# Two down products of a gated MLP, moved one pass later in three of sixteen passes

## The chip, the cores and the metric

One Trainium2 chip, one of its cores. TensorE (PE, its weight loads PEld), VectorE (DVE), ScalarE (ACT), GpSimd (POOL) and SyncE (SP) each run their own list of instructions in order and wait for each other through semaphores. The metric is the device time of one execution, in microseconds (us).

## The reference

`x` and `ctx` are (16, 256, 512): 16 batches of 256 tokens, width 512.

```python
x = x + tanh(g_xattn) * mlstm(layernorm(x), ctx, ctx, ...)   # 8 heads, decay matrix per head
h = layernorm(x)
scores = softmax(h @ router_w.T); top 2 of 16 experts
y = sum over the two experts of gate * ((silu(h @ Wg[e]) * (h @ Wu[e])) @ Wd[e])
s = (silu(h @ shared_gate) * (h @ shared_up)) @ shared_down  # 512 -> 512 -> 512, all tokens
x = x + tanh(g_ffn) * (y + s)
```

The change concerns `s`, the shared expert, and in it the last product, by `shared_down`.

## The kernel before

The kernel has three phases. In the first (to about 600 us) the 16 batches go through a software pipeline of passes; in the second (to about 1027 us) 79 tiles of 128 routed rows go through the experts; in the third the expert results are gathered and added, and the shared expert of the "late" batches is computed.

Pass `t` of the first phase works on four batches at once: F = t+1 (turn the context and x, gate rows), A = t (the attention of its 8 heads: `spread`, `scores_pair`, `pv`), G = t-1 (second layer norm, `turn`, router) and H = t-2 (ranks and slots of the routing, and the shared expert). The order is written out by hand in a function `step` for each engine, so every engine's instruction list is fixed. On PE a pass begins with `scores_pair(A, 0)` and has the sixteen gate products (`gates_pe`, L1030) about in its middle; I call what lies ahead of them the first half of the pass and what lies behind them the second half, and count times from them.

The shared expert of one batch is four `shared(b, m)` (24 matmuls of 128x256 each, L1125; they need DVE and ACT behind them for silu) and two `shared_down(b, j)` (12 matmuls of 128x512 each, L1136, one for each 128 tokens; DVE adds the result to `base_out`, L1618). Each product has three terms, since the operands are split in a high and a low part. `shared(b, 0)` and `(b, 1)` stand at the end of pass b+1, `(b, 2)` and `(b, 3)` in the first half of pass b+2, and both `shared_down` in the second half of pass b+2.

Batches 9, 11, 13 and 15 are `LATE`: their shared expert is left for the third phase. So passes 11, 13, 15 have no `shared(H, 2)`, `shared(H, 3)` and no `shared_down`, and passes 10, 12, 14 have no `shared(G, 0)`, `shared(G, 1)`. `EARLY` is all other batches, `LAST` = 14, `SH` numbers the early ones. Behind pass 15 stands a `drain`.

All products of the shared expert but `shared(b, 1)` and one of batch 14 use PSUM bank 7 (`FF`); `shared_down(b, 1)` waits until DVE has read `shared_down(b, 0)` out of it, and `shared(next, 0)` until DVE has read both. `spread(A, h)` waits until ACT has made the decay of head h-2, `pv(A, h)` until DVE has multiplied scores and decay (L1455), `columns` (L1042) until DVE has copied the logits. DVE's list has, in the first half of a pass: `h_stats(G)`, heads 0 and 1, `keep(H, 1)`, `norm_front(F, 0)`, `shared(H, 2)`, `center(G)`, heads 2 and 3, `x2_add`, `out_pair(A, 0)`, `norm_front(F, 1)`, `shared(H, 3)`, `x2_stats(G)`, top, heads 4 and 5, and `post_norm(G)` (L1525, for which PE's `turn(G, 0)` waits).

Of the kernel before, what the change touches and what calls it, by code (L numbers as in the profile page):

```python
# [44 lines left out]
LATE = (9, 11, 13, 15)  # L45
EARLY = tuple(b for b in range(B) if b not in LATE)
SH = {b: n for n, b in enumerate(EARLY)}
LAST = EARLY[-1]
LATE_TILES = len(LATE) * ST
YRING = 4  # L50
LATE_LOADS = [9, 16]
# [33 lines left out]
def flamingo_kernel(nc, x, ctx_in, g_xattn, g_ffn, igate_w, igate_b, fgate_w, fgate_b, ln_scale,  # L85
# [10 lines left out]
    with ExitStack() as stack:  # L96
# [163 lines left out]
        def gu_bank(b, m):  # L260
            return MB[0] if b == LAST and m == SC - 1 else GU[m]

# [714 lines left out]
        def _(pe):  # L977
# [135 lines left out]
            def shared(b, m):  # L1113
                pe.wait_ge(shared_in.sem, shared_in.upto(SHARED_PIECES - 1))
                pe.wait_ge(x2lo_made.sem, x2lo_made.upto(b.n))
                if m == 0:
                    pe.wait_ge(base_made.sem, base_made.upto(SH[b.n] - 1))
                elif b.n == LAST and m == SC - 1:
                    pe.wait_ge(decay_made.sem, decay_made.upto(B - 1))
                elif m > 1:  # L1120
                    pe.wait_ge(sh_act_made.sem, sh_act_made.upto(SH[b.n], 1 if m == 2 else 3))
                for at, w in ((0, sh_gate), (S, sh_up)):
                    for c in range(DC):
                        for p, (w_part, x_part) in enumerate(PARTS):
                            last = mm(gu_bank(b.n, m)[:, at:at + S], w[:, w_part, c, m * P:(m + 1) * P], x2nT[:, x_part, c, :],  # L1125
                                      start=(c + p == 0), stop=(c == DC - 1 and p == 2))
                last.then_inc(sh_made.sem, 1)
# [17 lines left out]
            def step(t, front=True, attend=True, route=True, rest=True):  # L1145
                F, A, G, H = t + 1, t, t + -1, t + -2
                inner, rest = rest, rest and H.n in SH
                mix = route and G.n in SH
                if attend:
                    scores_pair(A, 0)  # L1150
                    spread(A, 0)
                    spread(A, 1)
                if rest:
                    shared(H, 2)
                if front:
                    turn_ctx(F, 0)
                if attend:
                    spread(A, 2)
                    spread(A, 3)
                    pv(A, 0)  # L1160
                    pv(A, 1)
                    scores_pair(A, 1)
                if front:
                    turn_ctx(F, 1)
                if rest:
                    shared(H, 3)
                if front:
                    turn_x(F, 0)
                if attend:
                    spread(A, 4)  # L1170
                    spread(A, 5)
                    scores_pair(A, 2)
                if front:
                    turn_x(F, 1)
                if attend:
                    pv(A, 2)
                    pv(A, 3)
                if front:
                    gates_pe(F)
                if attend:  # L1180
                    spread(A, 6)
                    spread(A, 7)
                if route:
                    turn(G, 0, front)
                if rest:
                    shared_down(H, 0)
                if inner and route:
                    rank(H, front, attend)
                if attend:
                    pv(A, 4)  # L1190
                    pv(A, 5)
                if route:
                    turn(G, 1, front)
                if rest:
                    shared_down(H, 1)
                if attend:
                    scores_pair(A, 3)
                if route:
                    router(G, front)
                if mix:  # L1200
                    shared(G, 0)
                if attend:
                    pv(A, 6)
                    pv(A, 7)
                if route:
                    logits_pe(G)
                if mix:
                    shared(G, 1)
                if front:
                    columns(F, route)  # L1210
# [146 lines left out]
        def _(dve):  # L1357
# [237 lines left out]
            def shared(b, m):  # L1595
                dve.wait_ge(sh_tanh_made.sem, sh_tanh_made.upto(SH[b.n], m + 1))
                dve.wait_ge(sh_lo_made.sem, sh_lo_made.upto(SH[b.n], m - 1))
                v.scalar_tensor_tensor(sh_act[:, m % 2, :], silu_t[:, :], 1.0, gu_bank(b.n, m)[:, 0:S], ALU.add, ALU.mult
                                       ).then_inc(sh_silu_made.sem, 1)
                dve.wait_ge(sh_silu_made.sem, sh_silu_made.upto(SH[b.n], m + 1))  # L1600
                v.scalar_tensor_tensor(sh_act[:, m % 2, :], sh_act[:, m % 2, :], 0.5, gu_bank(b.n, m)[:, S:2 * S],
                                       ALU.mult, ALU.mult).then_inc(sh_act_made.sem, 1)
# [39 lines left out]
            def step(t, ahead=True, front=True, attend=True, route=True, rest=True, split=False):  # L1642
                N, F, A, G, H = t + 2, t + 1, t, t + -1, t + -2
                inner, rest = rest, rest and H.n in SH
                mix = route and G.n in SH
                if route:
                    h_stats(G)
                if attend:
                    head(A, 0)
                    head(A, 1)  # L1650
                if rest:
                    keep(H, 1)
                if split:
                    piece(0)
                if front:
                    norm_front(F, 0)
                if rest:
                    shared(H, 2)
                if route:
                    center(G)  # L1660
                if attend:
                    head(A, 2)
                    head(A, 3)
                if split:
                    piece(1)
                if route:
                    x2_add(G)
                if attend:
                    floor(A)
                    out_pair(A, 0)  # L1670
                if split:
                    piece(2)
                if front:
                    norm_front(F, 1)
                if split:
                    piece(3)
                if rest:
                    shared(H, 3)
                if route:
                    x2_stats(G)  # L1680
                if rest:
                    keep(H, 2)
                if inner and route:
                    top(H)
                if attend:
                    head(A, 4)
                    head(A, 5)
                if split:
                    piece(4)
                if route:  # L1690
                    post_norm(G)
                if attend:
                    out_pair(A, 1)
                if rest:
                    keep(H, 3)
                if split:
                    piece(5)
                if front:
                    read_gates(F)
                if inner and route:  # L1700
                    choose(H)
                if route:
                    turn(G, 0)
                if ahead:
                    stats(N)
                if rest:
                    shared_down(H, 0)
                if inner and route:
                    rank(H)
                if attend:  # L1710
                    out_pair(A, 2)
                if route:
                    turn(G, 1)
                if front:
                    rows(F)
                if rest:
                    shared_down(H, 1)
                if inner and route:
                    slots(H)
                if attend:  # L1720
                    head(A, 6)
                    head(A, 7)
                if front:
                    rows_end(F)
                if mix:
                    shared(G, 0)
                if route:
                    keep_logits(G)
                if attend:
                    out_pair(A, 3)  # L1730
                if mix:
                    keep(G, 0)
                    shared(G, 1)
                if front:
                    columns(F)
                if inner and route:
                    weigh(H)
# [215 lines left out]
```

## Time and profile before

| | us |
|---|---|
| median of 3 runs (lowest, highest) | 1143.31 (1141.41, 1145.24) |
| profiled execution, device time | 1135.05 |
| its span | 1133.2 |
| PE busy | 1025.1 (90%) |
| DVE busy | 761.3 (67%) |
| ACT busy | 386.4 (34%) |
| POOL busy | 419.3 (37%) |
| mean granted clock of PE | 0.949 |

The share of PE in the chain that ended last is 80%. Shares over the whole span say little of three passes of 34 us each; what counts is what the engines wait for in passes 10 to 15, at 402.9 to about 583 us. The granted clock of PE has two levels, 1.00 (2.4 GHz) and 0.50 (1.2 GHz); a stretch in which it changes shows a value between them.

### The profile page before, as it was taken

The page shows a single profiled execution, that of the slowest core. Times are in us where ns is not written, and L with a number is a line of the kernel's source. Part 1 is how long each engine was busy: PE and PEld are TensorE (multiplying, and loading weights), DVE is VectorE, ACT ScalarE, POOL GpSimd, SP SyncE. Part 2 cuts the span into 40 slices and gives each one's busy share as a digit, 9 for nine tenths or more (in the row PEclk, how much of TensorE's full clock was granted, in tenths as well). Part 3 has the DMA queues.
Part 4 walks back from the last instruction along what each step waited for, and adds up shares of the span by engine and source line. Part 5 has one row for each costly group of instructions (what it writes and reads, how often), then busy time and mean ns, then how long its engine had stood idle before and what let it go on. Part 6 is the DMA issues. An engine that isn't in the chain of part 4 may idle for free.

```text
span 1133.2 us, 20738 instructions
## 1 busy us (share of the span) xinstructions
PE 1025.1 (90%) x6395; PEld 859.9 (76%) x6395; DVE 761.3 (67%) x1983; ACT 386.4 (34%) x854; POOL 419.3 (37%) x309
## 2 busy tenths in 40 slices
PE   4689999999999988989895599999999999999882
PEld 2578988898889877868684478888888888887661
DVE  2888889888888887878766544444444444444766
ACT  2644444444443444435421123233323333231010
POOL 4010221222112221222215536558656676204675
PEclk9889999999999998989976899999999999999986
DMA  7340210222012202120107744564555554836888
GB/s 259 149 164 1 76 71 9 82 75 76 20 56 76 75 38 80 52 94 38 75 38 260 265 135 167 176 207 158 170 195 193 168 176 149 325 112 186 285 288 272
DMA packets 60036, 155.60 MB, mean 137 GB/s; under 512 B 7296, under 2 KB 7296, under 8 KB 58016
## 3 DMA queue, kind: packets, MB, share of 16 engines
q0 software_dynamic: 18448, 69.22, 17.6%
q1 hardware_dynamic: 29008, 62.93, 16.1%
q10 hardware_dynamic: 12480, 22.16, 5.5%
q8 instruction: 59, 0.97, 0.4%
q14 instruction: 41, 0.34, 0.1%
HBM read 93.46 MB, written 60.82 MB: 136 GB/s over the span
## 4 chain that ended last, share of the span: by engine, by line
PE 80%; DVE 5%; issue 4%; DMA 4%; POOL 3%; ACT 2%; SPq 1%; ACTq 0%; POOLq 0%; DVEq 0%; another core or an unknown queue 0%
PE bank L1260 19%; PE bank L1125 12%; PE bank L1278 10%; PE bank L1030 5%; PE bank L1136 5%; PE bank L1053 4%; PE bank L993 4%; PE bank L1248 3%; POOL w_ring L694 3%; PE bank L1074 3%; PE bank L1077 3%; PE bank L1075 3%; PE bank L1322 2%; PE bank L1062 2%; PE bank L1269 2%
## 5 line engine op out<-in xcount | busy, mean ns | idle before, releaser
L1260 PE MATMUL bank<-w_ring,x2nT 128*128 x948 | 241.8, 404 | 1.7 <-DVE x2nT L1829 1.7
L1260 PEld LDWEIGHTS bank<-w_ring,x2nT 128*128 128x128 f32 x948 | 174.3, 191 | 37.7 <-issue 2.4
L1125 PE MATMUL bank<-x2nT,w_ring 128*128 128x256 f32 x1152 | 148.5, 285 | 0.0
L563 POOL DMA_INDIRECT routed_x<-x2n,slot_u x64 | 65.8, 1029 | 222.8 <-DVE slot_u L1593 207.0
L1125 PEld LDWEIGHTS bank<-x2nT,w_ring 128*128 128x128 f32 x1152 | 141.0, 191 | 0.3
L1811 DVE SCALAR_TENSOR_TENSOR ctxT<-ctxT,bank 128x256 f32<-128x256 f32 x79 | 33.3, 421 | 138.7 <-ACT ctxT L921 138.7
L1278 PE MATMUL bank<-w_ring,sh_actT 128*128 x474 | 123.7, 396 | 1.1 <-DVE sh_actT L1824 1.1
L648 POOL TENSOR_TENSOR w_ring<-area,one 128x3072 fp32r<-128x3072 f32 x14 | 74.2, 5303 | 115.5 <-PE bank L1278 115.5
L1278 PEld LDWEIGHTS bank<-w_ring,sh_actT 128*128 128x128 f32 x474 | 88.9, 188 | 22.5 <-issue 1.4
L651 POOL TENSOR_TENSOR w_ring<-area,w_ring 128x3072 fp32r<-128x3072 f32 x14 | 95.6, 6832 | 2.5 <-POOL w_ring L648 2.5
L921 ACT ACTIVATE ctxT<-bank 128x256 f32<-128x256 f32 x79 | 30.3, 384 | 189.9 <-PE bank L1260 189.9
L694 POOL DMA_INDIRECT w_ring<-routed_y,y_slot x64 | 66.5, 1039 | 34.9 <-issue 19.6
L1136 PE MATMUL bank<-w_ring,sh_actT 128*128 128x512 f32 x288 | 75.2, 411 | 1.3 <-issue 1.3
L1455 DVE SCALAR_TENSOR_TENSOR area<-bank,area 128x384 f32<-128x384 f32 x128 | 66.0, 551 | 14.5 <-PE bank L1053 7.8
L927 ACT COPY cs_in<-bank 128x512 f32<-128x512 f32 x79 | 46.3, 586 | 84.7 <-PE bank L1278 79.1
L1822 DVE CAST sh_actT<-bank 128x256 fp32r<-128x256 f32 x79 | 33.5, 424 | 60.9 <-PE bank L1269 60.9
L570 POOL TENSOR_TENSOR x_rstd<-x_var,minus_half 128x2 f32<-128x2 f32 x16 | 12.8, 797 | 152.4 <-DVE x_var L1518 152.4
L1053 PE MATMUL bank<-area,ctxT 64*128 64x256 f32 (+1 forms) x512 | 67.1, 379 | 0.0
L778 ACT ACTIVATE area<-bank,key_log 128x256 f32<-128x256 f32 x128 | 61.1, 478 | 10.8 <-PE bank L1064 10.2
L1136 PEld LDWEIGHTS bank<-w_ring,sh_actT 128*128 128x128 f32 x288 | 53.8, 194 | 13.0 <-issue 1.5
L1248 PE MATMUL bank<-ident,x2n 128*128 128x128 f32 x316 | 48.4, 277 | 12.5 <-issue 7.0
L1053 PEld LDWEIGHTS bank<-area,ctxT 64*128 64x128 f32 x512 | 51.0, 206 | 11.3 <-issue 5.5
(224 smaller groups left out, 2052.8 us busy)
## 6 DMA issues: line engine op xcount, KB each, us to landing
routed_y<-cs_in ACTq DMA_DIRECT2D x79, 256.0 KB, 2.3
x2n<-routed_x SPq DMA_DIRECT2D x75, 256.0 KB, 2.9
base_out<-in_x_dram SPq DMA_DIRECT2D x16, 512.0 KB, 5.0
cs_in<-in_ctx_dram SPq DMA_DIRECT2D x16, 512.0 KB, 4.0
area<-n_L_ffn_expert_gate_dram POOLq DMA_DIRECT2D x16, 512.0 KB, 4.7
area<-in_L_ffn_expert_up_dram POOLq DMA_DIRECT2D x16, 512.0 KB, 6.3
area<-n_L_ffn_expert_down_dram POOLq DMA_DIRECT2D x16, 512.0 KB, 7.7
out_dram<-base_out SPq DMA_DIRECT2D x32, 256.0 KB
```

The source lines that it names most:

```text
L563: pool.indirect_dma_start(out=routed_x, in_=x2n[:, b.par, j, :], in_offset=None, out_offset=bass.IndirectOffsetOnAxis(ap=slot_u[:, b.par, ...
L648: g.tensor_tensor(w_ring[:, k, 0, :], stage[k], one[:, :].to_broadcast([P, EW]), ALU.mult).then_inc(expert_hi_in.sem, 1)
L651: g.tensor_tensor(w_ring[:, k, 1, :], stage[k], w_ring[:, k, 0, :], ALU.subtract).then_inc(expert_in.sem, 1)
L694: pool.indirect_dma_start(out=y_in[k][:, c, :], in_=routed_y, out_offset=None, in_offset=bass.IndirectOffsetOnAxis(ap=y_slot[:, at:at + 1] ...
L778: s.activation(decay[:, k, 0:S], MB[k][:, 0:S], ACT.Exp, bias=key_log[:, b.par, 0, h:h + 1], scale=-1.0)
L1053: last = mm(QK[k][:, at:at + n], ctxT[half, b.par, q, frm:frm + P], xnT[half, b.par, q, S - n:S], start=True, stop=True)
L1125: last = mm(gu_bank(b.n, m)[:, at:at + S], w[:, w_part, c, m * P:(m + 1) * P], x2nT[:, x_part, c, :], start=(c + p == 0), stop=(c == DC - ...
L1136: last = mm(FF[:, :], sh_actT[:, x_part, m, j * P:(j + 1) * P], sh_down[:, w_part, m, :], start=(m + p == 0), stop=(m == SC - 1 and p == 2))
L1248: last = tr(bank[t.par][:, c * P:(c + 1) * P], xt[:, k, c * P:(c + 1) * P], ident[:, :])
L1260: last = mm(bank[2 + t.par][:, :], xtT[:, x_part, t.par, c * P:(c + 1) * P], w_gu[:, bass.ds(slot, 1), w_part, c, :].rearrange("p a i -> p ...
L1278: last = mm(bank[5 + t.par][:, :], act_aT[:, x_part, t.par, c * P:(c + 1) * P], w_dn[:, bass.ds(slot, 1), w_part, c, :].rearrange("p a i - ...
L1455: v.scalar_tensor_tensor(cmat[:, k, :], QK[k][:, 0:TRI], QK_SCALE, decay[:, k, :], ALU.mult, ALU.mult).then_inc(c_made.sem, 1)
```

## The change

`CARRY` are the early batches whose successor is late, without the last: 8, 10 and 12. Their two `shared_down` leave the second half of pass b+2 (10, 12, 14) and stand in the first half of pass b+3 (11, 13, 15), in the places where `shared(H, 2)` and `shared(H, 3)` stand in a pass whose H is early. PE's list and DVE's list are changed in the same way; ACT, POOL and SP are not.

```diff
+CARRY = tuple(b for b in EARLY if b + 1 in LATE and b != LAST)
 # PE, step
                 if rest:
                     shared(H, 2)
+                if t.n - 3 in CARRY:
+                    shared_down(H + -1, 0)
                 if front:
                     turn_ctx(F, 0)
...
                 if rest:
                     shared(H, 3)
+                if t.n - 3 in CARRY:
+                    shared_down(H + -1, 1)
                 if front:
                     turn_x(F, 0)
...
-                if rest:
+                if rest and H.n not in CARRY:
                     shared_down(H, 0)
...
-                if rest:
+                if rest and H.n not in CARRY:
                     shared_down(H, 1)
 # DVE, step
                 if rest:
                     shared(H, 2)
+                if t.n - 3 in CARRY:
+                    shared_down(H + -1, 0)
                 if route:
                     center(G)
...
                 if rest:
                     shared(H, 3)
+                if t.n - 3 in CARRY:
+                    shared_down(H + -1, 1)
                 if route:
                     x2_stats(G)
...
-                if rest:
+                if rest and H.n not in CARRY:
                     shared_down(H, 0)
...
-                if rest:
+                if rest and H.n not in CARRY:
                     shared_down(H, 1)
```

## Rows read from the trace of the kernel before

**Rows 1.** Engines by stretch: us, busy (instructions) per engine, PEclk, DMA share, GB/s.
```profile
365.94:402.91 36.97, 36.97 (x292) 32.41 (x292) 32.43 (x95) 16.41 (x39) 7.63 (x9) 1.00 0.16 58
402.91:437.17 34.26, 30.46 (x196) 24.30 (x196) 28.80 (x92) 13.98 (x32) 8.21 (x9) 0.85 0.26 93
437.17:471.38 34.21, 31.59 (x267) 28.12 (x268) 27.67 (x83) 16.11 (x38) 6.58 (x7) 1.00 0.14 48
```
**Rows 2.** Chain that ended last: start us, us, engine, tile, line.
```profile
392.51 0.44 PE bank L993 x4
...
402.91 3.58 PE bank L1030 x16
...
407.61 2.81 PE bank L1136 x12
...
437.17 3.58 PE bank L1030 x16
...
539.89 3.58 PE bank L1030 x16
```
**Rows 3.** Timeline, pass 10 behind its gate products: start us, us, instruction, idle before.
```profile
413.72 0.42 DVE L1417 SCALAR_TENSOR_TENSOR f_row<-gates,f_row 8x256 f32<-8x256 f32 x1
...
415.94 0.71 DVE L1618 SCALAR_TENSOR_TENSOR base_out<-bank,tanh_g,base_out 128x512 f32<-128x512 f32 x1
...
418.07 0.44 PE L1074 MATMUL bank<-area 128*128 128x65 f32 x2 [0.92 <-DVE area L1455]
...
420.65 0.28 PE L1042 MATMUL bank<-ident,key_max 40*128 40x40 f32 x2 [0.48 <-DVE logits L1530]
...
422.24 0.61 PE L993 MATMUL bank<-ident,cs_in 128*128 128x128 f32 x4
```
**Rows 4.** Timeline, pass 11 behind its gate products.
```profile
446.06 0.58 ACT L728 CAST x2nT<-bank 128x512 fp32r<-128x512 f32 x1
...
447.40 0.41 DVE L1417 SCALAR_TENSOR_TENSOR f_row<-gates,f_row 8x256 f32<-8x256 f32 x1
447.42 1.20 PE L1100 MATMUL bank<-x2nT,router_wT 128*128 128x256 f32 x8 [2.12 <-DVE x2nT L1613]
```
**Rows 5.** Engines by stretch, columns as in Rows 1: where PEclk falls, holds and returns.
```profile
422.00:426.00 4.00, 2.32 (x25) 1.93 (x23) 3.87 (x11) 2.64 (x8) 3.65 (x5) 1.00 0.51 152
442.00:446.00 4.00, 2.94 (x28) 2.54 (x28) 3.67 (x14) 3.92 (x8) 0.00 (x0) 1.00 0.00 0
426.00:436.00 10.00, 9.28 (x48) 7.59 (x48) 7.38 (x24) 3.77 (x10) 0.69 (x1) 0.51 0.54 207
...
562.00:566.00 4.00, 4.00 (x24) 3.48 (x23) 1.76 (x3) 1.35 (x4) 0.27 (x1) 0.59 0.00 0
582.00:586.00 4.00, 4.00 (x31) 4.00 (x30) 0.74 (x2) 0.36 (x1) 2.82 (x3) 0.85 0.32 129
```
**Rows 6.** Chain that ended last, single products at either clock.
```profile
400.19 0.85 PE bank L1053 x8
...
427.14 1.58 PE bank L1053 x8
...
609.98 1.02 PE bank L1109 x4
...
1087.65 4.94 PE bank L1322 x12
```
**Rows 7.** Timeline, pass 15.
```profile
566.13 1.02 DVE L1455 SCALAR_TENSOR_TENSOR area<-bank,area 128x384 f32<-128x384 f32 x2 [2.37 <-PE bank L1053]
...
573.85 1.12 PE L993 MATMUL bank<-ident,x2n 128*128 128x128 f32 x4
...
575.91 0.67 PE L1074 MATMUL bank<-area 128*128 128x65 f32 x2
...
578.50 1.06 PE L993 MATMUL bank<-ident,x2n 128*128 128x128 f32 x4
...
581.08 2.07 PE L1100 MATMUL bank<-x2nT,router_wT 128*128 128x256 f32 x8
```

## The prediction

> **What bounds the kernel now.** I read the page first: PE is busy for 90% of the span and has 80% of the chain. That holds for the passes with all products: pass 9 to 10 (from one block of gate products to the next) takes 36.97 us with PE busy in all of it at clock 1.00 [rows 1]. Then I cut the span at the gate products, which the chain shows once in each pass [rows 2]. From pass 10 to 11 it takes 34.26 us, PE is busy for 30.46 of them, and the mean clock is only 0.85; from 11 to 12 it takes 34.21 us at clock 1.00 [rows 1]. (12 to 13 and 13 to 14 repeat these two to 0.1 us.) Nearly 12 us of PE work are absent in the first of them (four `shared`), and the time is shorter by only 2.7 us. So in the stretch that the change touches PE alone is not the bound: it waits for ACT and DVE in the second half of pass 10, and in the first half of pass 11 it runs 10 us at 1.2 GHz.
>
> All times below are counted from the gate products of pass 10 (402.91), 11 (437.17) and 14 (539.89), each called g.
>
> **Second half of passes 10, 12, 14: the products leave.** Two `shared_down`, 2.81 us each [rows 2], and two additions of DVE, about 0.7 us each [rows 3], go. What is late next is already in the trace: the second half of pass 11 has no down products. There the second turn of x2n waits for ACT (its cast begins at g+8.89), the router for DVE after 2.12 us of idleness, and DVE begins `rows` at 447.40, g+10.23 [rows 4]; in pass 10 it is 413.72, g+10.81 [rows 3]. So of 5.62 us of PE work taken away, 0.58 us come out. Behind that DVE has the scans, the second addition of the down product, slots and heads 6, 7; without the addition (0.65 us of it beyond the scan that it overlaps) `pv(6)` starts at 15.16 - 0.58 - 0.65 = g+13.93 instead of g+15.16 (418.07) [rows 3]. That is 1.23 us, and all that this half can give. PE idles for the rest: 2.1 us ahead of the router, as in rows 4, and then from the router's end (g+11.45) to g+13.93, another 2.5 us.
>
> At clock 1.00 `pv(6)` to `columns` is 420.65 - 418.07 = 2.58, and `columns` to the end of `spread(1)` 422.24 - 420.65 = 1.59 [rows 3], so `shared_down(8, 0)` would begin at g+18.1.
>
> **The clock.** It fell at about 426.2 in the kernel before. What PE did ahead of it: from 422 to 426 it was busy for 2.32 us of 4.00. From 442 to 446 it was busy for 2.94 of 4.00, and the clock held [rows 5]. In the changed pass 10 the stretch g+8 to g+14 has only the router in it, 1.2 us of some 5.9: much sparser than the one behind which the clock fell, and it comes 10 us earlier, in the second half where products were taken away. I therefore expect the fall at g+10 to g+13, and the return in the solid work of scores, spreads and the down product; it was back 10 us after the fall last time, and after 20 us in pass 15 (562 to 583) [rows 5].
>
> What stands ahead of the down product then runs at 1.2 GHz. A pair of `pv` takes 578.50 - 575.91 = 2.59 us, the logits 1.02, with 0.46 from them to `columns` 4.07 in all instead of 2.58. `scores_pair` takes 1.58 instead of 0.85, two spreads about 1.1 (twice the 0.5 left of the 1.59, an estimate), `columns` 0.3: 3.0 instead of 1.59 [rows 3, 6, 7]. So the first down product begins at 13.93 + 4.07 + 3.0 = g+21.0. It takes 2.81 us at 2.4 GHz; at 1.2 GHz the nearest row, 12 products of 128x512 that ran mostly at 0.50, has 4.94 [rows 2, 6]. Its end E is between g+23.8 and g+25.9; I take the middle between a return at its start and one at its end, a little to the early side since scores and spreads ahead of it are solid too: E = g+24.7.
>
> **First half of passes 11 and 13: the products arrive.** In pass 9, from the end of `shared(H, 2)` (392.51) to the gate products (402.91) it takes 10.40 us, bound by PE all the way, with `shared(H, 3)` in the place that the second down product now takes, of the same length [rows 2]. DVE's additions (0.7 us each) replace two silu steps and a `keep` of 0.4 each there, so DVE stays behind PE as in pass 9. The next gate products begin at 24.7 + 10.4 = g+35.1, against g+34.26: **+0.8 us**, bounds -0.1 (E = 23.8) and +2.0 (E = 25.9). Twice, for batches 8 and 10: +1.6.
>
> **Pass 15.** No F there, so it is not bound by PE work but by DVE and by PE at half clock. Now DVE's heads 2 and 3 begin at 566.13, g+26.24. Afterwards: E = 24.7, two spreads 0.6, a pair of `pv` 1.33, `scores_pair(1)` 0.85 and 0.2 to DVE give g+27.7, 1.46 later. From there DVE's list to `post_norm` (573.85 for PE's turn, 7.72 later) gets one addition more, 0.71: turn(G, 0) at g+36.1 instead of 33.96, +2.2. Behind it PE went at 1.2 GHz to the router at 581.08 [rows 7], and since PE again waits for DVE between g+33.4 and g+36.1 I keep that. So **+2.2 us**, bounds +1.3 and +3.4, and if these last 9.3 us ran at full clock 2.6 less (half of pv, turn, scores and router), so -1.3. The drain hangs on it one for one.
>
> **Hidden or free.** Nothing waits for `base_out` of 8, 10, 12 before `shared(next, 0)`, which comes 11 us behind the gate products of pass 11. ACT's `keep(10, 0)` waits for both downs of batch 8 and stands behind them too. No DMA is added or moved: context and x for two passes on are released by turns in the first half as in pass 9, and no instruction of POOL or SP is passed. If that cover were gone, the cost would be the whole of a load, 4 to 5 us; pass 9 has the same order and no such wait.
>
> **Sum.** 0.8 + 0.8 + 2.2 = +3.8 us on the profiled 1135.05, 1138.9. The profiled execution is 8.26 us under the median of the runs; the difference is carried over: 1143.31 + 3.8 = **1147.1**. With all bounds of these terms: -0.1 - 0.1 - 1.3 = -1.5 to 2.0 + 2.0 + 3.4 = +7.4, so 1141.8 to 1150.7.
>
> **Rivals.**
> *The clock holds (faster).* Then the first down begins at g+18.1, E = 20.9, the next gate products at g+31.3: -2.95 us, twice. In pass 15 heads 2 and 3 begin at g+23.9, 2.3 earlier, minus the addition 0.7: -1.6. Together -7.5, **1135.8**. For it speaks that the clock held over 2.12 us of idleness in pass 11 [rows 4]; against it that the dense `shared(G, 0)` followed there at once, while here 2.5 us more of idleness follow. It decides at the fall: it must not come before the first down.
> By the Trainium skill (TensorE: Matmul & The Clock Gate, "Part 1: The HAM clock gate") the array is throttled behind a stretch of idleness and released by sustained activity. Taken at its word, gaps that always have a router or a pair of `pv` between them would not throttle it, and this rival's 1135.8 would be the time; the trace disagrees, since the clock fell with PE busy for 2.32 of 4.00 us.
>
> *The fall comes, but the clock is back before the down product (same).* E = 23.8, each of the two passes -0.1, pass 15 +1.3: **1144.4**. Scores and spreads (2.7 us at half clock) would have to be enough to bring it back; in rows 5 PE was busy for 9.28 of 10 us before it came back, which speaks against it, but it comes back somewhere in such work.
>
> *The clock stays down past the first down (slower still).* Then turn, spreads, pv, scores and turn behind it take 3.5 us more, half of the second down 1 us: E = 25.9 and 4.5 on it, +6.5 for each of two passes, and pass 15 +3.4 + 2.5: +19, **1162**. Against it: five us without a gap.
>
> **How the numbers follow.** The forecast has 0.62, the clock back early 0.18, the clock holding 0.14, the long stay 0.06. A measurement of this kernel can tell about 0.3%, 3.4 us, from no change. The forecast lies just above that bound: of its 0.62 I put 0.35 above and 0.27 within. Slower 0.35 + 0.06 = 0.41; same 0.27 + 0.17 = 0.44; faster 0.14 + 0.01 = 0.15. Where the clock falls hangs on how gaps happen to lie in an execution, so the case before may itself move by a us or two; the range takes in the rival that is faster, nearly, and the upper bound with 1 us more: 1137 to 1152.
>
> **What would show it.** Right: in the changed kernel `pv(6)` of pass 10 at g+13.9; a clock of 0.50 from about g+10..13 to about g+23; the first L1136 of pass 11 at g+21 and over 3 us long; gate products of pass 11 at g+35.1; heads 2, 3 of pass 15 at g+27.7. Wrong: PEclk 1.00 between g+8 and g+18 (the first rival), or the gate products of pass 11 under g+33.

## The result, and the profile after

The changed kernel takes 1146.72 us in the median of 20 runs (1143.19 to 1154.82), the kernel before in the same series 1143.41 (1138.49 to 1151.49). The ratio is 1.0041, 95% interval [1.0021, 1.0061]: +4.7 us, between +2.4 and +7.0 (the two medians are 3.3 us apart). The forecast was 1147.1, +3.8 us. The profiled execution of the changed kernel took 1151.72 us, its span is 1149.9 us. It is 16.7 us over the profiled execution of before, and most of that is not the change: its gate products of pass 10, up to which nothing is changed, come 4.6 us later already, and 7 us come behind the router of pass 15. So here too the stretches between gate products are compared, not the spans. Line numbers are a little higher in the changed kernel: its L1032, L1102 and L1138 are L1030, L1100 and L1136 of before, and DVE's are six higher.

Engines by stretch, after, columns as in [rows 1]: gate products of pass 10 to those of 11, then 11 to 12, 12 to 13, 13 to 14.

```profile
407.46:442.98 35.52, 30.83 (x196) 25.34 (x196) 28.45 (x86) 13.68 (x31) 7.57 (x9) 0.81 0.25 89
442.98:477.19 34.21, 31.59 (x267) 28.12 (x268) 28.48 (x88) 16.32 (x39) 7.09 (x8) 1.00 0.14 48
477.19:512.04 34.85, 29.30 (x195) 24.05 (x196) 28.36 (x87) 13.68 (x31) 7.44 (x9) 0.85 0.21 76
512.04:547.74 35.70, 33.09 (x268) 29.61 (x268) 30.39 (x91) 16.31 (x39) 7.50 (x9) 0.95 0.08 31
```

The first stretch was 34.26 us in [rows 1]. It has the same 196 matmuls and now takes 35.52; the clock's mean went from 0.85 to 0.81. The second is unchanged. The fourth is 1.5 us longer than its like in the kernel before, by a short fall of the clock. Such a fall also comes in an execution of the kernel before (below), so this trace alone can't put it down to the change.

Timeline of pass 10 behind its gate products (g = 407.46), after; the answer to [rows 3, 4].

```profile
417.69 0.41 DVE L1423 SCALAR_TENSOR_TENSOR f_row<-gates,f_row 8x256 f32<-8x256 f32 x1
...
417.71 2.08 PE L1102 MATMUL bank<-x2nT,router_wT 128*128 128x256 f32 x8 [2.12 <-DVE x2nT L1619]
...
421.38 0.69 PE L1076 MATMUL bank<-area 128*128 128x65 f32 x2 [1.60 <-DVE area L1461]
...
425.65 0.41 PE L1044 MATMUL bank<-ident,key_max 40*128 40x40 f32 x2 [0.48 <-DVE logits L1536]
...
428.42 2.06 PE L1138 MATMUL bank<-w_ring,sh_actT 128*128 128x512 f32 x4
```

Read it against the forecast: `rows` begin at g+10.23 (forecast g+10.23), `pv(6)` at g+13.92 (13.93), the first down product at g+20.96 (21.0). PE sits idle ahead of the router for 2.12 us and ahead of `pv(6)` for 1.60 (forecast 2.5 at full clock). The router takes 2.08 us instead of 1.20 [rows 4], so the clock was already down.

Engines in 415.46 to 421.46, g+8 to g+14, after.

```profile
415.46:421.46 6.00, 2.29 (x13) 1.86 (x9) 4.77 (x13) 2.87 (x6) 0.00 (x0) 0.66 0.00 0
```

PE was busy for 2.29 of 6.00 us, much of that only because the router ran at half clock. The clock fell at g+9.9 and came back at g+23.6, inside the first down product. In passes 12 and 14 it fell at g+11.9 and g+13.0.

Chain that ended last, after.

```profile
407.46 3.58 PE bank L1032 x16
...
428.67 3.99 PE bank L1138 x12
...
436.44 2.79 PE bank L1138 x12
```

The chain counts a product from the end of the one before it, so the first carried product begins 0.25 us later here (g+21.2) than in the timeline. It takes 3.99 us, the second 2.79. The first ends at 432.66, E = g+25.2 (forecast 24.7), and the gate products of pass 11 follow 10.3 us later (forecast 10.4).

Timeline of pass 15 (g = 547.74), after; the answer to [rows 7].

```profile
575.61 1.02 DVE L1461 SCALAR_TENSOR_TENSOR area<-bank,area 128x384 f32<-128x384 f32 x2 [0.72 <-PE bank L1055]
...
579.10 0.74 DVE L1624 SCALAR_TENSOR_TENSOR base_out<-bank,tanh_g,base_out 128x512 f32<-128x512 f32 x1
...
583.77 0.66 PE L995 MATMUL bank<-ident,x2n 128*128 128x128 f32 x4 [1.71 <-DVE x2n L1531]
...
585.70 0.20 PE L1089 MATMUL bank<-chosen,before_b 128*128 128x16 bf16 x1 [1.28 <-DVE taken_mid L1564]
...
588.43 1.06 PE L995 MATMUL bank<-ident,x2n 128*128 128x128 f32 x4
...
591.00 1.41 PE L1102 MATMUL bank<-x2nT,router_wT 128*128 128x256 f32 x8
```

Heads 2 and 3 begin at g+27.87 (forecast 27.7; before 26.24), `turn(G, 0)` at g+36.03 (forecast 36.1; before 33.96) and waits 1.71 us for DVE. The router begins at g+43.3 instead of g+41.2: +2.1, forecast +2.2. The clock was not down all through this stretch, as it was in the kernel before: it came back at g+23.2 and fell again at g+36.9, behind `turn(G, 0)`, which takes 0.66 us instead of 1.12. The time from `turn(G, 0)` to the router is 7.2 us in both kernels, since PE then waits 1.28 us for DVE.

### The profile page after: what moved, and what is told of

Read it like the earlier page. It is cut to its first block, busy times and chain, and to the rows that moved or that the text cites. A ratio compares the mean times of both kernels' runs of the same rounds, so it can differ in the third digit from the quotient of the medians.

```text
span 1149.9 us, 20738 instructions
## 1 busy us (share of the span) xinstructions
PE 1032.3 (90%) x6395; PEld 865.9 (75%) x6395; DVE 763.5 (66%) x1983; ACT 386.0 (34%) x854; POOL 419.7 (36%) x309
## 4 chain that ended last, share of the span: by engine, by line
PE 79%; issue 6%; DVE 4%; DMA 4%; POOL 3%; ACT 2%; SPq 1%; another core or an unknown queue 0%; ACTq 0%; POOLq 0%; DVEq 0%
PE bank L1266 19%; PE bank L1127 12%; PE bank L1284 9%; PE bank L1138 5%; PE bank L1032 5%; PE bank L1055 4%; PE bank L995 4%; PE bank L1254 3%; POOL w_ring L696 3%; PE bank L1076 2%; PE bank L1077 2%; PE bank L1079 2%; PE bank L1064 2%; DMA routed_x<-xn 2%; PE bank L1328 2%
## 5 line engine op out<-in xcount | busy, mean ns | idle before, releaser
L1266 PEld LDWEIGHTS bank<-w_ring,x2nT 128*128 128x128 f32 x948 | 174.9, 191 | 38.0 <-issue 2.4
L1138 PE MATMUL bank<-w_ring,sh_actT 128*128 128x512 f32 x288 | 77.4, 420 | 1.3 <-issue 1.3
L1138 PEld LDWEIGHTS bank<-w_ring,sh_actT 128*128 128x128 f32 x288 | 55.7, 201 | 13.6 <-issue 1.5
L1076 PE MATMUL bank<-area 128*128 128x65 f32 x256 | 52.0, 287 | 10.9 <-DVE area L1461 10.9
L1254 PE MATMUL bank<-ident,x2n 128*128 128x128 f32 x316 | 48.9, 278 | 13.7 <-issue 7.3
```

The source lines that it names most:

```text
L1076: mm(HO[:, r:r + VW], cmat[:, k, 0:P], v_aug[:, b.par, 0, h, :], start=True, stop=True)
L1138: last = mm(FF[:, :], sh_actT[:, x_part, m, j * P:(j + 1) * P], sh_down[:, w_part, m, :], start=(m + p == 0), stop=(m == SC - 1 and p == 2))
L1254: last = tr(bank[t.par][:, c * P:(c + 1) * P], xt[:, k, c * P:(c + 1) * P], ident[:, :])
L1266: last = mm(bank[2 + t.par][:, :], xtT[:, x_part, t.par, c * P:(c + 1) * P], w_gu[:, bass.ds(slot, 1), w_part, c, :].rearrange("p a i -> p ...
```

## Experiments

Each run's ratio is to the kernel before in runs of the same series, and the microseconds behind it are that ratio worked out on 1143. g is always the block of gate products that opens a stretch.

**Fill the emptied places** (fill_gaps). A helper `fill(n)` issues n matmuls of 128x512 into bank 7, read by nobody.

```diff
+                if rest and H.n in CARRY:
+                    fill(8, acts=H)
                 if route:
                     router(G, front)
+                if rest and H.n in CARRY:
+                    fill(9)
```

> The changed kernel, and in the second half of passes 10, 12, 14 PE gets idle work in the two places where it waits: 8 products of 128x512 ahead of the router and 9 behind it, into bank 7, whose content nobody reads. The output is the same. Theory A (the clock): the change is slow because the emptied second half lets the clock fall at g+10; filled, the clock holds, pv(6) still starts at about g+13.9 to g+14.3, the first down product at about g+18.4 instead of g+21.0, and gate products of pass 11 at g+31.3 to g+32 instead of g+35.5. Pass 15's router ends about 3 us earlier than in the changed kernel. Together 7 to 11 us under the changed kernel, 3 to 7 us under the kernel before. Rival B (the place: DVE's additions and bank 7 delay heads 2 and 3 whatever the clock does): the fillers only add work, the gate products of pass 11 stay at g+35 or later, time as the changed kernel or slower.

Measured: 1141.49 us, ratio to before 0.9963 [0.9933, 0.9994], so -4.2 us, and 8.9 under the changed kernel's ratio. Engines by stretch: 10 to 11, 11 to 12, and g+13.9 to g+21.9.

```profile
411.15:442.57 31.42, 30.02 (x212) 24.05 (x213) 27.80 (x86) 13.80 (x31) 7.81 (x9) 1.00 0.28 102
442.57:478.30 35.73, 33.12 (x268) 29.64 (x268) 30.18 (x89) 16.31 (x39) 7.31 (x8) 0.95 0.12 45
425.00:433.00 8.00, 7.44 (x57) 6.53 (x58) 7.22 (x25) 2.62 (x7) 6.76 (x7) 1.00 0.35 135
```

With 17 more matmuls issued the first stretch takes 31.42 instead of 35.52 us, at clock 1.00 (PE busy for 7.44 of the 8 us behind `pv(6)`), and the first down product begins at g+18.1, where the forecast put it for a clock that holds; that rival had 31.3. Order, places and DVE's work are those of the changed kernel. 12 to 13 takes 31.59 us. So the whole loss in these two stretches, and the gain that was within reach, hang on the clock: shown, and rival B falls. The fillers did not hold the clock everywhere. It fell for 3.4 us at g+10.4 in pass 11 and at g+11.4 in pass 13 (where no fillers stand), and at g+16.7 in pass 14; the router of pass 15 begins at g+40.9, 2.4 us earlier than in the changed kernel, and ends 1.7 us earlier and not the 3 expected.

**The same work in the kernel before** (before_fill). Behind `spread(A, 1)` of passes 11, 13, 15: `fill(12)`.

```diff
                 if rest:
                     shared(H, 2)
+                if t.n - 3 in (8, 10, 12):
+                    fill(12, bases=H + -1)
                 if front:
                     turn_ctx(F, 0)
```

> The kernel before, and in the first half of passes 11, 13, 15, behind spread(1), PE gets 12 products of 128x512 that nobody reads, 2.8 us of work where a down product stands in the changed kernel. Output the same. Theory A: the sparse stretch at g+19 to g+23 is filled and the clock, which fell there at g+23.3, holds; the 10 us at 1.2 GHz become 5 us of work and the rest is bound by DVE; gate products of pass 11 at g+31 to g+32.5 instead of g+34.3, 2 us in each of two passes and 2 to 4 in pass 15: 5 to 8 us under the kernel before, although 8.4 us of work are added. Rival B (the work in the first half is what costs): PE work is added on the path, gate products of pass 11 at g+36 to g+37, 5 to 8 us over the kernel before.

Measured: 1137.50 us, 0.9951 [0.9917, 0.9984], -5.6 us.

```profile
410.74:443.93 33.19, 30.30 (x208) 24.39 (x208) 27.80 (x86) 13.89 (x31) 7.83 (x9) 0.95 0.27 96
478.13:509.76 31.63, 28.73 (x208) 23.19 (x208) 27.82 (x87) 13.89 (x31) 7.71 (x9) 1.00 0.24 84
```

Useless work makes the kernel before faster. Where the clock held throughout, 12 to 13 takes 31.63 us; in 10 to 11 it fell at g+18.1 for 3.4 us and the stretch takes 33.19, over the 32.5 expected. The fall came ahead of the fillers' place, so they could not prevent it.

**One product stays, one goes** (one_late).

```diff
                 if t.n - 3 in CARRY:
-                    shared_down(H + -1, 0)
+                    shared_down(H + -1, 1)
...
                 if mix:
                     shared(G, 0)
+                if rest and H.n in CARRY:
+                    shared_down(H, 0)
                 if attend:
                     pv(A, 6)
```

(the same is done in DVE's list, and the other carried call goes)

> Of the two down products of 8, 10, 12 the first stays in its own pass, but stands behind the router, where shared(G, 0) stands in passes with an early G; only the second goes one pass later, to the place of shared(H, 2). Theory A: the product behind the router fills 2.5 us of idleness, the clock holds or falls at g+10 to g+12 and is back by g+14 since dense work follows (as in the second half of pass 11); pv(6) at about g+14.4; the carried product at g+18.5 to g+19; then 7.6 us of PE work or about 9 of DVE's: gate products of pass 11 at g+30 to g+32.5. 6 to 12 us under the changed kernel, 2 to 7 under the kernel before. Rival B (every carried product costs by its place): half of the loss stays, about 2 us over the kernel before.

Measured: 1135.34 us, 0.9927 [0.9890, 0.9963], -8.4 us. Stretches 10 to 11, 11 to 12 and 13 to 14:

```profile
403.55:435.53 31.98, 27.17 (x196) 22.29 (x196) 28.62 (x86) 13.71 (x31) 7.60 (x9) 0.95 0.29 99
435.53:469.74 34.21, 31.59 (x268) 28.11 (x268) 28.39 (x88) 16.35 (x39) 7.10 (x8) 1.00 0.13 48
502.19:537.84 35.65, 33.03 (x268) 29.56 (x268) 30.37 (x91) 16.34 (x39) 7.50 (x9) 0.95 0.08 31
```

The same 196 matmuls take 31.98 us, with a fall of 3.4 us only (g+9.8 to g+13.2): the clock was back 0.9 us into the product behind the router, where the changed kernel has no product and stayed down to g+23.6. In passes 12 and 14 the clock held there and fell at g+18.7 and g+18.9, again for 3.4 us; 12 to 13 takes 32.45 us. It beats both kernels, by more than expected (2 to 7 us under before, 6 to 12 under the changed one): it is 13.0 us under the changed kernel's ratio.

**Batch 12 alone** (only12). `CARRY = (12,)`.

> CARRY is (12,) alone: passes 10 to 13 are as before, passes 14 and 15 as in the change. By the forecast's terms pass 15 alone costs +2.2 us and each of the other two +0.8; then this kernel is +1 to +2.5 us over the kernel before, the router of pass 15 ends at g+44.5 to g+45.5 (counted from the gate products of pass 14), against g+43.3 in the kernel before, and gate products of pass 11 are at about g+34.3. If pass 15 costs nothing, the router ends at g+43 to g+43.5.

Measured: 1144.54 us, 1.0003 [0.9972, 1.0034], which tells nothing of 2 us. Its stretches do: 10 to 11, and gate products of pass 14 to 43.5 us behind them.

```profile
403.53:435.50 31.97, 27.73 (x196) 21.98 (x196) 27.80 (x86) 13.78 (x31) 7.84 (x9) 0.95 0.27 99
539.80:583.28 43.48, 35.81 (x219) 28.91 (x218) 32.15 (x104) 14.16 (x34) 7.43 (x8) 0.77 0.12 49
```

The router of pass 15 starts at the end of the second stretch, g+43.5, as in the changed kernel, and ends at g+45.0, within the 44.5 to 45.5 expected: the loss of pass 15 comes without the other two. The first stretch was not expected: passes 10 and 11 are those of the kernel before, and take 31.97 us and not 34.26. The clock fell at g+23.5, where it fell at g+23.3 in the first trace of before, but for 3.4 us instead of 10.2.

**Carried products of one matmul** (thin_down). Inside the loop over m of PE's `shared_down`:

```diff
+                    if b.n in CARRY:
+                        if m == SC - 1:
+                            last = mm(FF[:, :], sh_actT[:, 0, m, j * P:(j + 1) * P], sh_down[:, 0, m, :],
+                                      start=True, stop=True)
+                        continue
```

> The changed kernel, but each of the six carried down products does one of its 12 matmuls; the other 11 (with the values that they would add for batches 8, 10, 12) are left out. 2.6 us of PE work less in each place, 15.5 us in all; waits and DVE's additions stay. Theory A (the clock): the product itself was the solid work that brought the clock back; without it the clock, fallen at g+10 to g+13, stays at 0.50 through most of the first half of passes 11 and 13: the product's place is reached at g+21 as before, and the gate products of pass 11 come at g+33.5 to g+36, as late as with the whole products (35.5), if not later. Time within 5 us of the changed kernel. Rival B (what costs is PE work in the first half): gate products of pass 11 at 35.5 - 5.2 = g+30.3, 5 us less in each of three passes, 15 us under the changed kernel, 1131 to 1134.

Measured: 1140.27 us, 0.9983 [0.9951, 1.0015]. Stretch 10 to 11, and g+9.6 to g+23.6 of it:

```profile
407.43:439.38 31.95, 25.99 (x173) 21.25 (x174) 27.61 (x82) 13.80 (x31) 7.40 (x8) 0.79 0.26 99
417.00:431.00 14.00, 11.24 (x56) 9.91 (x57) 11.17 (x32) 4.43 (x10) 6.60 (x7) 0.51 0.31 114
```

And one wait of PE behind the place of the second product:

```profile
437.45 0.66 PE L995 MATMUL bank<-ident,xn 128*128 128x128 f32 x4 [0.77 <-DVE xn L1416]
```

A miss for both. The place is reached at g+21.0 again, with the clock down since g+9.9; but the clock comes back at g+23.6 without the product, as it did with it, so I was wrong that the product is needed for that: what PE did there was turn, spreads and `pv`. The stretch is 3.6 us shorter than with whole products, near the 3.99 us of the first. Nothing comes out for the second: from the end of the first carried product to the gate products it takes 10.2 us, and 10.3 with whole products, since turn and spreads run at half clock up to g+23.6 and PE then waits, here 0.77 us for DVE. The time is 6.6 us under the changed kernel's ratio, more than theory A's 5 and far less than rival B's 15. Of 15.5 us of PE work left out, 1.9 us under before remain (interval -5.6 to +1.7), which can't be told apart from what fill_gaps gives with work added.

**Both in their own pass, behind router and logits** (both_behind). `shared_down(H, 0)` stands as in one_late, both carried calls go, and in both lists:

```diff
                 if mix:
                     shared(G, 1)
+                if rest and H.n in CARRY:
+                    shared_down(H, 1)
```

> Both down products of 8, 10, 12 stay in their own pass but stand where shared(G, 0) (behind the router) and shared(G, 1) (behind the logits) stand in passes with an early G. Theory A: the second half holds the clock or has one short fall, pv(6) at about g+14.4, the second product puts columns at g+19.5 to g+20; then the first half of pass 11 is as sparse as in the kernel before, and the clock falls there at g+24 to g+26 for 3 to 10 us: gate products of pass 11 at g+33 to g+35. So 0 to 2 us better than the kernel before in each pass at most, and 3 us or more over the kernel one_late, which shows that the second product is worth more in the first half. Rival B (carried products cost by their place): as good as one_late or better.

Measured: 1143.26 us, 0.9983 [0.9958, 1.0007]. 10 to 11 and 11 to 12:

```profile
402.60:434.75 32.15, 26.49 (x196) 20.94 (x196) 27.15 (x86) 13.67 (x31) 7.58 (x9) 1.00 0.27 99
434.75:470.44 35.69, 33.08 (x268) 29.60 (x268) 30.18 (x89) 16.31 (x39) 7.28 (x8) 0.95 0.13 46
```

The time came as expected, 6.4 us over one_late's ratio, with intervals that just overlap, but not for the reason given: the clock held in the first half of pass 11, so 10 to 11 is as short as in one_late. In this trace 11 to 12 and 13 to 14 both have a short fall (35.69 instead of 34.21), but 13 to 14 has it in one_late too, and in the kernel before it comes now and then (below). That the second product is worth more in the first half is not shown by these stretches.

**one_late with fillers ahead of the router** (one_late_fill), in passes 10 to 15.

```diff
+                if rest and H.n in CARRY:
+                    fill(8, acts=H)
+                if t.n - 3 in CARRY:
+                    fill(8, bases=H + -1)
                 if route:
                     router(G, front)
```

> one_late, and ahead of the router of passes 10 to 15 PE gets 8 products of 128x512 (1.9 us) that nobody reads, in the 2.1 us in which it waits there for DVE. Output the same. Theory A: the falls at g+10 to g+12 in passes 11, 13 (and 10) that cost 1.45 us each in executions where they come (35.7 instead of 34.2 from one block of gate products to the next) go: 0 to 4 us under one_late, 34.2 us for 11 to 12 and 13 to 14 in every execution, 31.5 to 32.5 for 10 to 11. Rival B (the fillers delay the router): the router starts at g+10.8 instead of g+10.3, and each pass is 0.4 longer, 2 us over one_late.

Measured: 1132.70 us, 0.9922 [0.9883, 0.9961], -8.9 us; against one_late (0.9927) it can't be told apart by time. 10 to 11 and 11 to 12:

```profile
403.56:434.45 30.89, 27.93 (x204) 22.49 (x204) 27.23 (x86) 13.79 (x31) 7.56 (x9) 1.00 0.29 103
434.45:468.67 34.22, 33.67 (x276) 29.55 (x276) 28.43 (x88) 16.32 (x39) 7.08 (x8) 1.00 0.14 47
```

12 to 13 takes 31.05 and 13 to 14 34.22 us. The clock held from pass 10 to g+29.5 of pass 14, the router begins at g+10.3 as ever, and 10 to 11 is the shortest of the changed orders seen. This is one execution; that the short falls stay away in every one, as theory A has it, is not shown.

**Both kernels again**, two more executions of each.

> The kernel before once more, unchanged, for a second execution of its passes. The look at only12, whose passes 10 and 11 are those of the kernel before, had 31.97 us from the gate products of pass 10 to those of 11 with a fall of 3.4 us, where the first trace of the kernel before had 34.26 with a fall of 10.2 us. Theory A (the length of the low stretch decides, and it varies from execution to execution): the 10 to 11 and 12 to 13 stretches are each near 32 or near 34.3, and 11 to 12 and 13 to 14 near 34.2 or, with a fall at g+10 to g+12, near 35.7. Rival B (a fixed schedule): 34.26, 34.21, 34.31, 34.20 again.

> As before_b, a third execution: 10 to 11 near 32 or 34.3; 11 to 12 near 34.2 or 35.7; the router of pass 15 between g+40 and g+41.5.

> The changed kernel once more, unchanged. Theory A: the fall at g+10 to g+13 in passes 10, 12 and 14 comes in every execution, since the emptied second half does not depend on chance; the first down product at g+21.0 (20.5 to 21.1); gate products of pass 11 and 13 at g+34.3 to g+36; pass 15's router at g+43 to g+44. So about 1 to 3.5 us over the kernel before in each, depending on which state the latter is in. If the clock holds in one of them, that stretch is near 31.3.

> As after_b, a third execution: falls at g+10 to g+13 in passes 10, 12, 14, stretches 10 to 11 and 12 to 13 of 34.3 to 36, 11 to 12 and 13 to 14 near 34.2 or 35.7.

10 to 11 in two more executions of the kernel before (b, then c), then in two of the changed one:

```profile
410.32:441.19 30.87, 27.66 (x195) 22.01 (x196) 27.80 (x86) 13.78 (x31) 7.81 (x9) 0.94 0.28 103
```

```profile
402.51:436.91 34.40, 30.47 (x196) 24.31 (x196) 28.82 (x92) 13.98 (x32) 8.34 (x9) 0.85 0.26 93
```

```profile
410.39:446.47 36.08, 30.64 (x195) 25.00 (x196) 28.45 (x86) 13.70 (x31) 7.56 (x9) 0.81 0.25 88
```

```profile
402.45:437.82 35.37, 29.82 (x196) 24.41 (x196) 28.44 (x86) 13.68 (x31) 7.56 (x9) 0.86 0.25 90
```

All stretches, in us (first the traces shown above, then b, c):

| | before | changed |
|---|---|---|
| 10 to 11 | 34.26, 30.88, 34.39 | 35.51, 36.09, 35.37 |
| 11 to 12 | 34.21, 35.70, 34.21 | 34.21, 34.21, 35.70 |
| 12 to 13 | 34.31, 34.23, 34.37 | 34.85, 35.18, 35.65 |
| 13 to 14 | 34.20, 34.20, 34.21 | 35.70, 35.69, 34.21 |
| 14 to the router of 15 | 41.25, 41.07, 41.36 | 43.33, 43.50, 42.87 |
| sum | 178.2, 176.1, 178.5 | 183.6, 184.7, 183.8 |

The means of the sums are 177.6 and 184.0, 6.4 us apart, within the interval of the timed difference. In all nine carrying passes the clock fell between g+9.9 and g+13.0, the first down product began at g+21.0, and the clock came back between g+22.1 and g+24.8, inside that product.

The kernel before varies more. Its order of passes 10 to 13 also stands in only12, which makes eight stretches of the kind 10 to 11. In six the clock fell at g+22.1 to g+23.3 for 10.2 us and they took 34.2 to 34.4 us. In two it fell for 3.4 us only: at g+18.0 (before_b, 30.88 us, under the 32 expected) and at g+23.5 (only12, 31.97 us). Of its eight stretches of the kind 11 to 12, two had a short fall at g+11 to g+12 and took 35.70. In the changed kernel, fill_gaps, before_fill, one_late, thin_down and both_behind together ten of sixteen had it; in one_late_fill, with fillers ahead of each of these routers, neither of two. That is too few to say whether the orders differ in it.

The same sum in the single trace of each other kernel is 175.4 (fill_gaps), 174.7 (before_fill), 175.3 (one_late), 172.0 (one_late_fill), 174.9 (thin_down), 177.3 (both_behind) and 179.8 us (only12), against 177.6 before and 184.0 changed. The order of the timed results is much the same, but one_late's timed gain of 8.4 us is more than the 2.3 us that its trace shows in these stretches. Its runs lie anywhere between 1129.7 and 1147.3 us, and where the rest comes from is open.

## Why the prediction was right

*What bounds it.* The forecast said that PE alone was not the bound in these stretches, and that what leaves the second half frees 0.58 + 0.65 us and no more. That held to 0.01 us (`pv(6)` at g+13.92).

*The clock.* It fell early in all nine passes, so the chance of 0.62 seems low in hindsight. That the fall makes the loss is shown by fill_gaps: the same order with the clock held goes from 35.52 to 31.42 us. The comparison that the forecast leaned on was weaker than it looked. It took the sparse stretch 442 to 446 of pass 11, where the clock held, as the safe side, but in an execution of the same kernel (before_b) the clock fell at about g+11 of the same pass, 2.2 us behind that stretch. And of the solid work that was to bring the clock back the product is not needed: thin_down has the return at g+23.6 without it.

*The first down product.* Start 21.0 as forecast. Its length was a little under-sized: 3.99 in the first pass, 3.33 and 3.84 in the others, where E = 24.7 stood for 3.7. E came at g+25.2, 24.5 and 25.1.

*Passes 11 and 13.* Forecast +0.8 each. The changed kernel's six stretches have a mean of 35.4 (forecast 35.1), but the kernel before's six have 33.7 instead of the 34.26 that I took from one trace. So the term is about +1.7 each: 0.3 from E and what follows it, 0.5 because one of the six stretches of before had the short fall and took 30.88. The forecast had taken the outcome with the long fall, which is the commoner one; against it alone the change costs 1.1 to 1.2 us. This is the step of the sum that was mis-sized, and the sum of stretches, +6.4, is over the +3.8 for this reason and for one more: a short fall in 11 to 12 or 13 to 14 came in three of six stretches of the changed kernel and in one of six of the kernel before, 0.5 us in the mean for each of the two. With three traces of each I can't say whether that is chance. That the measured median (1146.72) lies only 0.4 us from the forecast 1147.1 is partly luck: by the ratio the change costs 4.7 us, by the stretches 6.4, and the forecast had 3.8.

*Pass 15.* +2.1 in the first pair of traces and +2.0 in the mean of three, +2.2 forecast, by the terms named: heads 1.6 later (forecast 1.5), DVE's list up to `turn(G, 0)` 0.4 longer (forecast 0.7 for the addition), the rest at the same length. For that rest the forecast kept half clock throughout; the first 0.9 us of it ran at full clock and PE waited for DVE instead, so the term came out right.

*The rivals.* The clock holding did not come in this kernel; forced by fillers it gives the stretch that it was priced at (31.3 forecast, 31.42). The clock back before the product and the clock down past it did not come either: in all nine passes it came back inside the product. Nothing of what I had called hidden came out: `shared(next, 0)`, `keep` and the loads of context wait for nothing new, and 11 to 12 takes the 34.21 us that it took before where no short fall comes.

## What to carry to other kernels

When work is taken out of a stretch in which TensorE already waits for other engines, ask what the emptied stretch does to TensorE's clock before asking what the receiving stretch costs. Here 5.6 us of products bought 1.2 us where they left, and then half clock for 10.2 or 13.7 us. Of the orders tried, the one with a product in each of two gaps did best (0.9927), better than both in one half (1.0041 and 0.9983). Take the price of a clock fall from several executions, since one trace shows one outcome of it.

## What the runs showed of the hardware that was not expected

Matmuls whose result nobody reads made the kernel faster: 36 of them (12 in each of three passes) took 5.6 us off the kernel before (interval 1.8 to 9.5).

And the same instructions up to the gate products of pass 10 took 402.5 us in one execution and 410.3 in another, of both kernels alike (402.51 and 410.32 before, 402.45 and 410.39 changed). The granted clock differs at the start: in the first 100 us its mean is 0.91 in the short ones and 0.81 in the long ones, and 0.86 in the first trace of the changed kernel, with 407.46. That is 8 us, more than the change itself; why it differs no run here tells. Behind the router of pass 15, where all thirteen traces have the same instructions, the time to the end varies by as much: 551.2 to 562.1 us.
